# Attention with a mixture of experts: token rows scattered to their slots in HBM and turned by VectorE, in place of gathered rows turned by TensorE

## The reference

```python
xn = layernorm(x)
q, k, v = split(xn @ w_qkv.T + b_qkv)                # attention within each batch
s = softmax(q @ k.T / sqrt(512)) @ v @ w_out.T + b_out
vals, idx = top_k(xn @ router_w + router_b, 2)       # 8 experts, 2 of them for each token
w = softmax(vals)
h = silu(xn @ expert_w[e] + expert_b[e])             # for each of the token's two experts
y = xn + (sum of w * h) @ proj_w + proj_b
out = x + s * silu(norm_w * y / rms(y))
```

## Time and profile before

| | |
|---|---|
| median of 3 runs | 532.55 us (531.38 to 532.72) |
| the profiled execution | 533.14 us, of which the profile's span is 531.4 us |
| TensorE busy | 514.9 us, 97% of the span |
| VectorE, ScalarE, GpSimd busy | 267.9, 201.2, 199.7 us |
| mean granted clock of TensorE | 0.992 of full speed |
| HBM | 56.13 MB read, 24.90 MB written |

### The profile page before, as it was taken

How to read it: one execution, slowest core, us unless ns; L and a number is a source line. 1 busy time by engine, 2 the same in 40 slices (tenths; PEclk the granted TensorE clock), 3 DMA queues, 4 the chain that set the end, 5 groups by cost and what they waited for, 6 DMA issues and landing times.

```text
span 531.4 us, 7656 instructions
## 1 busy us (share of the span) xinstructions
PE 514.9 (97%) x2454; PEld 414.7 (78%) x2455; DVE 267.9 (50%) x428; ACT 201.2 (38%) x300; POOL 199.7 (38%) x316
## 2 busy tenths in 40 slices
PE   4999999999999999899999999999999999999995
PEld 2488667887888888788888888888888888888884
DVE  2557232856138255664444444444574854567552
ACT  0265542222034254543333333323363552426550
POOL 3053210000007874243333330435457765266143
PEclk9999999999999799999999999999999999999999
DMA  8761277000100488857755554869523541242202
GB/s 265 270 239 39 93 243 299 0 21 20 41 0 1 178 278 297 283 192 228 245 172 165 165 161 145 301 237 307 169 79 100 198 146 52 83 152 65 79 37 83
DMA packets 37130, 81.40 MB, mean 153 GB/s; under 512 B 4128, under 2 KB 4144, under 8 KB 37104
## 3 DMA queue, kind: packets, MB, share of 16 engines
q1 hardware_dynamic: 27312, 50.60, 26.8%
q0 software_dynamic: 7920, 27.03, 16.6%
q10 hardware_dynamic: 1872, 3.41, 2.2%
HBM read 56.13 MB, written 24.90 MB: 152 GB/s over the span
## 4 chain that ended last, share of the span: by engine, by line
PE 91%; DVE 2%; DMA 2%; issue 1%; POOL 1%; ACT 1%; SPq 0%; ACTq 0%; DVEq 0%
PE ab L1385 19%; PE ab L1387 19%; PE ab L1386 19%; PE tp L1391 9%; PE sc L1385 6%; PE sc L1387 6%; PE sc L1386 6%; PE sc L1411 3%; DMA y_scratch<-yt 1%; DMA raw_o<-in_w_out_t 1%; PE tp L1562 1%; PE sc L1472 1%; PE ab L1419 1%; PE sc L1475 1%; DVE yt L1253 0%
## 5 line engine op out<-in xcount | busy, mean ns | idle before, releaser
L1385 PE MATMUL ab<-W,st_h 128*128 x156 | 64.5, 414 | 1.7 <-DVE st_l L1118 1.7
L1387 PE MATMUL ab<-W,st_l 128*128 x156 | 61.4, 394 | 0.0
L1386 PE MATMUL ab<-W,st_h 128*128 x156 | 60.9, 390 | 0.0
L863 ACT ACTIVATE yt<-yt 128x512 f32<-128x512 f32 x39 | 24.7, 632 | 75.9 <-DVE yt L1253 75.9
L1385 PE MATMUL sc<-xt_h,t_h 128*128 128x512 f32 x128 | 51.5, 403 | 0.0
L1387 PE MATMUL sc<-xt_h,t_l 128*128 128x512 f32 x128 | 50.9, 398 | 0.0
L1386 PE MATMUL sc<-xt_l,t_h 128*128 128x512 f32 x128 | 50.8, 397 | 0.0
L1118 DVE TENSOR_TENSOR st_l<-tp,st_h 128x512 fp32r<-128x512 f32 x40 | 27.7, 691 | 38.9 <-ACT st_h L859 29.2
L664 POOL DMA_INDIRECT y<-y_scratch,pos x32 | 31.0, 970 | 40.8 <-DMA y_scratch<-yt 20.6
L618 POOL TENSOR_TENSOR tile_hot<-in_tile,ids 128x640 fp32r<-128x640 f32 x2 | 6.5, 3242 | 90.0 <-DVE in_tile L1167 90.0
L1253 DVE TENSOR_TENSOR yt<-ab,bias_e 128x512 f32<-128x512 f32 x39 | 27.0, 692 | 26.2 <-PE ab L1387 22.1
(11 more groups left out here) (271 smaller groups left out, 1268.4 us busy)
## 6 DMA issues: line engine op xcount, KB each, us to landing
y_scratch<-yt SPq DMA_DIRECT2D x39, 256.0 KB
xb<-in_expert_w POOLq DMA_DIRECT2D x6, 1024.0 KB, 6.3
xn_scratch<-xs SPq DMA_DIRECT2D x16, 256.0 KB, 2.0
x<-in_x SPq DMA_DIRECT2D x16, 256.0 KB, 3.2
xb<-in_x SPq DMA_DIRECT2D x4, 512.0 KB, 8.6
xb<-in_x POOLq DMA_DIRECT2D x2, 1024.0 KB, 6.8
nw_scratch<-nw SPq DMA_DIRECT2D x1, 2048.0 KB, 13.1
mw_scratch<-mw SPq DMA_DIRECT2D x1, 2048.0 KB, 18.3
```

The lines of the kernel that those rows point to most:

```text
L863: nc.scalar.activation(yt[:, h, :], yt[:, h, :], ACT.Silu).then_inc(silu_d, 1)
L1385: nc.tensor.matmul(dst, lh, rh, start=start, stop=False)
L1386: nc.tensor.matmul(dst, lh, rl, start=False, stop=False)
L1387: return nc.tensor.matmul(dst, ll, rh, start=False, stop=stop)
```

## The change

The table of tokens and the gathers are gone. SP first reads the 16 row tiles back into SBUF (`load_to_send`, eight buffers in `xb1`) and fills all 39 slot tiles in HBM with zeros by three DMAs, 10.2 MB in all. Once the routing is known GpSimd sends each row tile twice by an indirect DMA to the slots `pos1` and `pos2`. SP then loads a slot tile with four DMAs, each of 32 partitions: partition 32a+s gets quarter a (128 features, 512 bytes) of the rows s, 32+s, 64+s and 96+s. VectorE turns the tile by one instruction with 32x32 blocks (`turn` in its program), reading every fourth feature, straight into `tp`. So feature 4p+c lies on partition p, and not feature 128c+p; all else that meets features on partitions follows: the raw expert weights are loaded as `(p c)`, with 8 KB in one piece per partition, and TensorE's weights in `fold_keys`, `key_weights`, `turn(g)` and the first fold are read with a stride of four elements (`every_fourth`). TensorE has no `turn_rows` or `turn_own` any more. The turning runs four tiles ahead of the matmuls instead of one, and `g_split` of tile i+2 waits for the matmuls of tile i. The early expert matrices are split at other places (`EARLY_AT`), and GpSimd does its half in quarters between the sends; the fourth `early_high`, ahead of the exponent of the last row tile of block 1, waits until all sends have landed, since its target lies on `xb1`.

```diff
@@ SP
+            def load_to_send(g):
+                if g >= GB:
+                    sp.wait_ge(sent[g % GB], 32)
+                sp.dma_start(sent_rows[:, g % GB, :], rows_g[home(g)]).then_inc(send_in[g % GB], 16)
+            def load_tile(i, q):
+                for a in range(4):
+                    sp.dma_start(rows[q][32 * a:32 * (a + 1), :].rearrange("p (r f) -> p r f", r=4),
+                                 rows_q[ds(i, 1), a, :, :, :].rearrange("o s r f -> s (o r) f")).then_inc(xg_in[q], 16)
+            def load_next(i, q):
+                sp.wait_ge(g_t, i - 3)
+                load_tile(i, q)
+            for q in range(4):
+                sp.wait_ge(xn_st[q], 4 * G)
+            for g in range(GB):
+                load_to_send(g)
+            sp.wait_ge(zero_set, 1)
+            for n in range(3):
+                w = slice(n * SLOT_TILES // 3, (n + 1) * SLOT_TILES // 3)
+                sp.dma_start(rows_t[:, w, :], zeros.to_broadcast([P, w.stop - w.start, D])).then_inc(zero_in, 16)
...
                 sp.wait_ge(ab_read, 2 + U["a", 0, j] + 1)
                 sp.dma_start(s_g[j], so[:, j % 2, :]).then_inc(so_st[j % 2], 16)
+                if 1 <= j <= 3:
+                    for g in range(GB + 2 * j - 2, GB + 2 * j if j < 3 else G):
+                        load_to_send(g)
+                if j == QB + 1:
+                    for g in range(GB):
+                        sp.wait_ge(sent[g], 64)
+                    for i in range(2):
+                        load_tile(i, i)
+                if j == QB + 2:
+                    sp.wait_ge(ptr_done, 1 + GB)
+                    for i in range(2, 4):
+                        load_tile(i, i)
+            for i in range(4, 8):
+                load_next(i, i % 4)
...
             for i in range(PEEL):
                 store_y(i, i % 2)
+                load_next(i + 8, i % 4)
...
@@ GpSimd
+            pool.wait_ge(zero_in, 48)
+            pool.wait_ge(routed, 1)
+            for g in range(G):
+                pool.wait_ge(send_in[g % GB], 16 * (g // GB + 1))
+                for pos in (pos1, pos2):
+                    pool.indirect_dma_start(slots_d, bass.IndirectOffsetOnAxis(pos[:, g:g + 1], 0),
+                                            sent_rows[:, g % GB, :], None).then_inc(sent[g % GB], 16)
+                if g < 3 * KC:
+                    early_low(g // KC, g % KC)
+            for c in range(KC):
+                early_low(3, c)
...
@@ ScalarE
+        EARLY_AT = ((0, 2), (0, 3), (1, 0), (1, 3))
...
+                if e == 0:
+                    act.wait_ge(routed, 1)
+                elif e == 1:
+                    for g in range(GB):
+                        act.wait_ge(sent[g], 64)
...
@@ VectorE
+            def turn(i, q, j, first=False):
+                dve.wait_ge(xg_in[q], 64 * (j + 1))
+                if not first:
+                    dve.wait_ge(g_lo, i - 1)
+                vec.transpose(tp[:, q % 2, :, :].rearrange("p c (r s) -> p c r s", r=4),
+                              rows[q].rearrange("p (r q c) -> p c r q", r=4, c=KC)).then_inc(g_t, 1)
...
                 pt_low(3)
                 if tail:
+                    dve.wait_ge(pt_lo, 1 + GB)
+                    turn(0, 0, 0, True)
+                    turn(1, 1, 0, True)
                     w_low(0)
                     w_low(1)
                 attn_out(2)
                 if tail:
                     g_low(0, 0)
+                    turn(2, 2, 0)
+                    g_low(1, 1)
+                    turn(3, 3, 0)
                     w_low(2)
                     w_low(3)
                 attn_out(3)
...
             for i in range(PEEL):
-                g_low(i + 1, (i + 1) % 2)
                 add_bias(i, i % 2, i < 2)
+                g_low(i + 2, i % 2)
+                turn(i + 4, i % 4, i // 4 + 1)
+                if i < LATE - AHEAD:
+                    w_low(i + AHEAD)
...
@@ TensorE
+            def every_fourth(row, n):
+                return row.rearrange("p (q c) -> p c q", c=KC)[:, n, :]
...
             for i in range(PEEL):
-                turn_rows(i + 1, (i + 1) % 4, (i + 1) // 4, i == 0)
                 expert(i, i % 2)
```

More of the change, by code:

```diff
@@ L181, in gated_attention_moe @@
         xbs = (xb, xb1)
[L182 to L185, removed]
+        sent_rows = xb1
+        zeros = xn[:, 0:1, :]
         with ExitStack() as a:
@@ L512, in _ @@
             sp.wait_ge(mw_st, 16)
[L513 to L516, removed]
[L517 to L519 removed]
+            for k in range(2 * KC):
                 load_key_weights(k)
@@ L629, in _ @@
-            for k in range(2):
-                number_tiles(k)
-            for k in range(3):
-                early_low(k)
-            def gather(i, q):
-                link(pool.tensor_copy(idx[:, q:q + 1], token[:, ds(i, 1)]))
-                pool.nop(nofuse=True)
-                pool.indirect_dma_start(rows[q], None, xn_d,
-                                        bass.IndirectOffsetOnAxis(idx[:, q:q + 1], 0)).then_inc(xg_in[q], 16)
-            for q in range(4):
-                pool.wait_ge(xn_st[q], 4 * G)
@@ L1262, in _ @@
                 add_bias(i, i % 2, i < 2)
-                if 1 <= i <= LATE - AHEAD:
-                    w_low(i + AHEAD - 1)
-            with dve.Fori(PEEL // 2, LOOPED // 2) as i:
-                for h in range(2):
-                    g_low(2 * i + h + 1, 1 - h)
-                    add_bias(2 * i + h, h)
-            for i in range(LOOPED, SLOT_TILES):
-                g_low(i + 1, (i + 1) % 2)
-                add_bias(i, i % 2)
+                g_low(i + 2, i % 2)
+                turn(i + 4, i % 4, i // 4 + 1)
+                if i < LATE - AHEAD:
+                    w_low(i + AHEAD)
+            with dve.Fori(PEEL // 4, LOOPED // 4) as i:
+                for q in range(4):
+                    add_bias(4 * i + q, q % 2)
+                    g_low(4 * i + q + 2, q % 2)
+                    turn(4 * i + q + 4, q, i + 1)
             def own_low(i):
@@ L1276, in own_low @@
                 vec.tensor_tensor(low, tp[:, i % 2, :, :], high, ALU.subtract).then_inc(g_lo, 1)
+            for i in range(LOOPED, SLOT_TILES):
+                add_bias(i, i % 2)
+                if i + 2 < SLOT_TILES:
+                    g_low(i + 2, i % 2)
+                else:
+                    own_low(i + 2)
+                turn(i + 4, i % 4, i // 4 + 1)
             def combine(p):
@@ L1442, in turn @@
                     pe.wait_ge(lo_done, g - 1)
-                transpose_tile(xs[:, g % 4, :], g % 2).then_inc(t_done, 1)
+                for c in range(KC):
+                    last = nc.tensor.transpose(tp[:, g % 2, c, :], every_fourth(xs[:, g % 4, :], c), ident[:, :])
+                last.then_inc(t_done, 1)
             def values(b, t):
```

234 lines of the change are left out of this document (72 added, 162 removed).

## The result

The changed kernel takes **537.42 us** (median of 4 runs), the kernel before 532.41 in the same job: a ratio of 1.0098, 95% interval 1.0073 to 1.0122. The profiled execution spans 535.7 us, 4.3 more than before. The forecast was 524.0, so its direction was wrong, though 537.4 lies within its range of 508 to 540.

A forecast was written before the change was run, and what follows sets the result against it. It took TensorE, busy 514.9 of 531.4 us, as the bound; -29.8 + 7 + 2.7 + 3.4 + 0 + 4 + 3 = -9.7 us gave a forecast of 524 us, 1.6% faster than 532.55, range 508 to 540.

The forecast's parts named there:

- (a): Token table's 32 small TensorE matmuls removed: 4.05 us, plus 2.8 for the slow clock behind them, together -6.8 us.
- (g): Stride of four in TensorE's weight reads (folds, key_weights, turn(g)): loads slower but nearly hidden, +3 us.
- (b): TensorE's 47 turns of slot tiles and batch 1 tiles removed, 0.49 us each: -23.0 us.
- (c): Sends hold block 1's last exponent: TensorE waits 7 us (0 to 13), plus 2.7 for the clock.
- (d): First expert tiles: late third and fourth tiles and VectorE's work delay expert 1 and tiles to 5: +3.4 us, bounds 0 and 7.
- (e): VectorE's turn of a slot tile takes 0.70 us (at most 1.38), covered by the matmuls: 0 us.
- (f): SP's queue in the expert loop: five or six issues a tile at 0.34 to 0.57 us beside TensorE's 2.72: +4 us.
- SP becomes the bound: Rival: at 0.66 us an issue SP's queue sets the tile step, +24 in place of +4, 543 us; chance 0.12.
- The rival built on full halving: Stride halves all readers: weight-load pairs 0.254 us, transposes 0.2, VectorE's turn 1.24 or more; 538 us; chance 0.12.

The follow-up runs named there:

- run 3: The kernel before with the stride of four in TensorE's weight reads alone; table, gathers and TensorE's turns of the slot tiles kept: 536.7 us, ratio 1.0084.
- run 1: Changed kernel with the fourth early_high, which waits for all sends, moved behind the attention blocks: 536.18 us, ratio 1.0105 to the kernel before.
- Run 2: Changed kernel with SP's loads of tiles 2 to 7 issued ahead of the stores of s that wait: 530.59 us, ratio 0.9973 to the kernel before.
- run 4: Changed kernel with VectorE's turn reading 32 neighbouring features, which breaks the match with the weights: 533.56 us, ratio 1.0041 to the kernel before.
- run 10: As run 7, but VectorE's turn reads 32 neighbouring features instead of every fourth: 522.48 us, ratio 0.9812 to the kernel before.
- run 7: Changed kernel, edits of run 1 and Run 2, folded-weight loads on ScalarE's queue, folded key weights stored in order of use: 522.41 us, ratio 0.9789.
- runs 8 and 9: On top of run 7, GpSimd's sends ahead of all low halves (552.69 us), or ahead of only the third and fourth early products' low halves (527.2 us).
- run 9: As run 7, but the third early product's low halves also stand behind the last send: 527.2 us, ratio 0.992 to the kernel before.

## Why the prediction was wrong, point by point

- **(a), the table, right in size, its clock not explained.** row_max(7) starts at 183.51, before 187.93. TensorE was 2.4 us late ahead of the table's place (177.87 against 175.46), which I put down to (g), so that is -6.8, as forecast. But the prediction took it that the small matmuls halve the clock, and run 3 passes the same 32 at full speed. What lowered the clock in the kernel before is open.
- **(b), the turns, right, a tenth smaller.** From tile 18 to 38 the step is 3.195 us before and 2.754 after, so 0.44 a tile where 0.49 was taken. The step is no longer TensorE's own, which the prediction named as what would make it wrong most of all: the chain there lies on SP's queue, whose 2.75 happens to be next to TensorE's 2.72.
- **(c), the sends, nearly right, in part by luck, and still wrongly placed.** First send 128.94 (128 forecast), first to last end 58.5 us (59), TensorE's wait 7.23 us (7), a stretch at half clock behind it. The first send was to wait for the zeros; it waited for the routing, whose last operation starts at 127.83, while the DMAs had gone idle by 124. The last send landed 7.3 us after the start of its issue, where 4.3 was taken. So TensorE had its probabilities at 197.0 and not at 194.7, and as it wanted them at 189.8 and not at 187.3, the two errors cancelled. What I missed is that the same sends also hold the first tiles' loads: run 1 takes the whole wait away and gains nothing that can be measured.
- **(d), the first tiles: the step that failed.** The prediction followed VectorE's order and put the third and fourth tile behind attn_out(2), but it followed SP's queue no further. The loads of tiles 4 to 7 stand behind the store of the last s, and that behind attn_out(3), which on VectorE stands behind the turns of tiles 2 and 3. So the loads were taken to overlap with expert 0, and did not. The nine tiles from expert 0 on were counted at 29.5 to 30 us and took 41.0: (d) is +14.4 where +3.4 was taken, twice its bound of 7. Run 2, which only reorders SP, gives back 1.25% or 6.7 us, and with run 1 in place the pair gives 2.2%, 11.6 us. The clock takes its share: each idle stretch of 4 to 7 us in the changed kernel has a stretch at half speed behind it (0.83 over 60 us).
- **(e), VectorE's turn: the term mis-sized.** 1.104 us instead of 0.70, within the bound of 1.38. In the changed kernel it costs 3 to 4 us (run 4), a part of the 14.4 above, presumably since VectorE is what the late loads are handed to; in run 10 it costs nothing that can be measured. The Trainium skill ("VectorE: DVE Perf Modes", section "The three transpose paths") gives 311 ns for 128x128 in bf16; the estimate of 1.24 us by it was nearer than mine, but run 4's 0.725 us for fp32 and neighbours shows that it is the stride that makes the difference, not the transpose.
- **(f), SP's queue: right mechanism, half again as large.** Four loads' issues are 1.74 to 1.86 us, some 0.45 each, where 0.34 to 0.57 was the span between its bounds. Six issues take 3.49 us a tile, 0.58 from start to start, where TensorE wants 2.72, so tiles 8 to 18 cost +6.1 over the turns' gain, where +4 was taken for all tiles. The prediction's own sum for 0.57 is 8.6 - 2.5 = 6.1: the upper bound held, and I took the middle. Five issues take 2.75 and just keep pace. The rival "SP becomes the bound" wanted 0.64 an issue, which was not reached, but the chain shows SP as the bound even so, at a step next to TensorE's.
- **(g), the stride, about right.** Where +3 was taken, the changed kernel shows +2.4 us ahead of the table's place. Run 3 has +4.8 by the medians (4.5 by the ratio), of which the rows give 2.9 ahead of the table and 1.0 behind tile 38 to the stride itself; the waits in its expert stage and the clock that didn't fall make up the rest. Weight loads became 312 ns, 66% longer, and still the pair's step grew only from 0.227 to 0.235 us, for the load lies under the product before it. The Trainium skill ("SBUF — State Buffer", section "Door 1: The DMA port swizzle") calls a stride of four fp32 free; the loads at 188 against 312 ns and the turns at 725 against 1,104 show that here it isn't, for these two readers. The rival built on full halving (0.254 a pair, 538 us) came out at the right time for the wrong reason: its pair step was not seen.

So one omission, (d), with the mis-sized turn of (e) in it, makes 11.0 of the 14 us; the rest is (f) and turns that save 0.44 us in place of 0.49. The forecast's range held, but by rivals whose mechanisms were not seen. The sum itself gives 522.8 for the median (523.4 less the 0.6 of the profiled execution), and I wrote 524 with no term for the difference. Taken out one by one the missed costs are mostly order and not work. That run 7, at 522.4 us, meets the forecast of 524.0 is luck, though: it has no wait at the exponent, no sixth issue and no stride in its key weights, for which the forecast had added 13.7 us and a part of (g), and its nine first tiles still take 36.9 us (205.05 to 241.94 on TensorE) and not 30. Still open is what ScalarE, VectorE and TensorE stood for in runs 8 and 9. No run here takes the row of sends apart any further, so a cause would be guesswork. Also left open is the rest of the wait ahead of expert 0 (4.00 us in run 7): run 9 was to remove it, and its stall covered the answer.

## What to carry to other kernels

When loads move to a queue that also holds stores, write out that queue's order past the change and ask of each store what it waits for: a load behind a store waits for everything that the store waits for, and if the store's producer stands behind that load's consumer, the latencies add up. Remove such waits together before judging any one of them, as one alone may only uncover its neighbour. Count issues per tile as a resource of their own: here SP's four-part loads cost 1.8 us of a tile's 2.7, with the store SP was level with TensorE, and one more DMA a tile made a tile 3.49 us. And when an edit gains nothing, see where its wait went: in run 1 the same 7 us stand ahead of the next experts.

## What of the hardware was not expected

- A stride of four fp32 lengthens TensorE's weight loads from 188 to 312 ns and VectorE's 128x512 block transpose from 725 to 1,104 ns; of the first little reaches the step of load and product, which grows by hardly 4% (2.72 to 2.82 us for twelve).
- VectorE's fp32 block transpose of 128x512 into PSUM takes 0.725 us if it reads neighbours, about what any 128x512 operation of this kernel takes there (0.69).
- TensorE's clock stood at 0.50 behind 32 small matmuls in the kernel before and at 1.00 behind the same 32 in run 3, so a stretch at half speed in one trace doesn't show its cause.
- 32 indirect sends in a row, 1.26 us apart, went with a standstill of ScalarE of 40.7 us whose releaser the profile doesn't name, 16 in a row with one of 11.9. For 28 and about 8 us of these the program's own wait was already fulfilled. In the other kernels, with a low half of 1.3 us behind each of the first twelve pairs and only the last eight sends in a row, there was none.
